# Turning the level tiles of x by transposing DMA transfers on SP instead of PE and DVE

## The reference

```python
x = x + tanh(g_xattn) * xattn(layernorm(x), ctx, ctx)     # softmax with a temperature from a small MLP on score statistics
y = layernorm(x)
# _bitlinear(a, w) = act_quant(a) @ weight_quant(w).T
# act_quant(a): scale = 127 / max|a| of the row; round(a * scale) / scale   (levels from -127 to 127)
# weight_quant(w): levels -1, 0, 1 by the mean of |w|
h = silu(_bitlinear(y, w_gate)) * _bitlinear(y, w_up)      # inner size 1024
x = x + tanh(g_ffn) * _bitlinear(h, w_down)
```

## Time and profile before

| | us |
|---|---|
| median of three runs | 788.13 |
| lowest, highest | 787.66, 788.53 |
| the profiled execution | 786.88 |
| its span from first to last instruction | 785.0 |

### The profile page before, as it was taken

One profiled execution on the slowest core, in us unless ns is written; L12 is line 12 of the kernel. 1 busy time (PEld: TensorE's weight loads), 2 busy tenths in 40 slices (PEclk: granted clock), 3 DMA queues, 4 the chain that ended last, 5 costly groups with the idle time before them and its releaser, 6 DMA issues.

```text
span 785.0 us, 20889 instructions
## 1 busy us (share of the span) xinstructions
PE 707.7 (90%) x7127; PEld 479.5 (61%) x7127; DVE 702.0 (89%) x1432; ACT 672.5 (86%) x1440; POOL 506.1 (64%) x1004
## 2 busy tenths in 40 slices
PE   7557899989999999999999999999999888879896
PEld 5334566767676766666666666676766566634453
DVE  5779799979899999998999999899999887889995
ACT  1469799999999999989999999999999987559884
POOL 4747657667777776766767676767675146546873
PEclk9667599999999999999999999999999999999998
DMA  9897856465567575667565758565755023238887
GB/s 213 191 256 165 189 140 134 115 124 132 138 125 146 123 145 127 147 118 154 118 151 125 151 120 142 125 154 115 153 111 116 13 73 101 67 74 183 184 178 193
DMA packets 148886, 108.49 MB, mean 138 GB/s; under 512 B 56991, under 2 KB 145183, under 8 KB 148767
## 3 DMA queue, kind: packets, MB, share of 16 engines
q1 hardware_dynamic: 143630, 101.98, 59.7%
q10 hardware_dynamic: 5152, 5.19, 2.7%
HBM read 49.54 MB, written 12.85 MB: 79 GB/s over the span
## 4 chain that ended last, share of the span: by engine, by line
PE 46%; ACT 20%; DVE 14%; issue 10%; POOL 7%; DMA 1%; ACTq 1%; SPq 0%; POOLq 0%; DVEq 0%
PE p_m L1458 9%; PE p_o L1380 8%; ACT ex L1228 7%; PE p_s L1360 7%; ACT pt L1218 6%; PE p_t L1401 6%; PE p_m L1439 5%; DVE stats L950 3%; PE p_m L1447 3%; DVE nm L969 2%; PE p_m L1431 2%; ACT L1218 2%; ACT L1254 2%; POOL kst L785 2%; PE p_m L1465 2%
## 5 line engine op out<-in xcount | busy, mean ns | idle before, releaser
L1228 ACT ACTIVATE ex<-p_s,nm 112x375 f32<-112x375 f32 x512 | 275.0, 616 | 12.4 <-DVE nm L969 12.4
L1218 ACT ACTIVATE pt<-p_t,ct 128x336 f32<-128x336 f32 x488 | 244.9, 574 | 29.1 <-PE p_t L1401 26.6
L950 DVE BATCH_NORM_STATS2 stats<-ex 112x6 f32<-112x375 f32 x512 | 252.4, 534 | 1.8 <-ACT ex L1228 1.8
L969 DVE TENSOR_REDUCE nm<-p_s 112x2 f32<-112x750 f32 x256 | 235.9, 922 | 2.3 <-PE p_s L1360 2.2
L1360 PE MATMUL p_s<-kst,qst 96*112 96x375 bf16 x512 | 156.1, 351 | 13.7 <-ACT ex L1228 7.7
L1401 PE MATMUL p_t<-qst,kst 99*128 99x112 bf16 x1464 | 115.3, 214 | 4.9 <-ACT pt L1218 4.2
L1401 PEld LDWEIGHTS p_t<-qst,kst 99*128 99x128 bf16 x1464 | 91.4, 98 | 43.9 <-issue 19.4
L1439 PE MATMUL p_m<-wv_sb,ctxt 128*128 128x256 f32 (+1 forms) x384 | 107.7, 404 | 5.0 <-DVE on L938 3.2
L1380 PE MATMUL p_o<-pt,va 128*32 128x112 f32 (+1 forms) x3072 | 101.6, 265 | 0.5 <-ACT ex L1228 0.5
L1458 PE MATMUL p_m<-ctxt,wk_sb 128*128 128x375 f32 x240 | 94.8, 519 | 1.7 <-DVE qf L918 1.1
L1360 PEld LDWEIGHTS p_s<-kst,qst 96*112 96x112 bf16 x512 | 67.0, 140 | 46.0 <-ACT ex L1228 36.3
(11 more groups left out here) (189 smaller groups left out, 1162.8 us busy)
## 6 DMA issues: line engine op xcount, KB each, us to landing
kst<-kp SPq DMA_DIRECT2D x378, 93.8 KB, 3.5
ctxt<-ctxt_dram SPq DMA_DIRECT2D x32, 375.0 KB, 4.2
qbounce<-qp SPq DMA_DIRECT2D x32, 168.0 KB, 2.5
qst<-qbounce SPq DMA_DIRECT2D x32, 168.0 KB, 3.6
qst<-qbounce SPq DMA_DIRECT2D x32, 112.0 KB, 3.4
xm<-x_dram SPq DMA_DIRECT2D x32, 112.0 KB, 2.3
x_dram<-x SPq DMA_DIRECT2D x32, 112.0 KB, 1.9
xt<-x_dram SPq DMA_DIRECT2D x28, 128.0 KB, 3.2
```

The lines of the kernel that those rows point to most:

```text
L950: last = nc.vector.bn_stats(stats[:, nb % RING, 2 * pb + i], ex[0:SQ, 2 * (t % 2) + i, :])
L969: nc.vector.tensor_reduce(nm[:, n % RING, 2 * p:2 * p + 2], p_s[t % 2][0:SQ, :, 0:SK], axis=AX.X, op=ALU.max, negate=True).then_inc(s_max, 1)
L1218: nc.scalar.activation(pt[:, (2 * r + i) % 8], st_home(r, i)[:, 0:KC * SQ].rearrange("k (c q) -> k c q", c=KC), ACT.Exp, scale=ct[:, nr % ...
L1228: nc.scalar.activation(ex[0:SQ, 2 * ((t - 1) % 2) + i, :], p_s[(t - 1) % 2][0:SQ, i, 0:SK], ACT.Exp, bias=nm[:, ne % RING, h:h + 1]).then_ ...
```

## The change

The PE transposes and the DVE copies of the level tiles are gone. SP issues one transposing transfer for each tile (`turn_group`), straight from `fxq` to `xqt(k)`, at the slot at which PE transposed before, and for the late groups at tiles 14 and 17. It waits for POOL's levels and for what the copy waited for. POOL waits for the landing of a group's transfers before it writes the buffer again. PE's gate product waits for the landing. Since p_t[0] is free in the tail, row 30's `ong` transposes ride there, and rows 30 and 31 have a bank each. Tile 0 stands behind slot 283 instead of 284, and `rows_scale` at slot 280 instead of 282.

```diff
-        last_ride = p_t[1][:, 0:C * SQ].rearrange("p (c q) -> p c q", c=C)
+        last_rides = [p_t[i][:, 0:C * SQ].rearrange("p (c q) -> p c q", c=C) for i in range(2)]
...
-            return last_ride if m5 == B - 1 else tail_ride if t >= TAIL else ride[t % 2]
+            return last_rides[m5 % 2] if m5 >= B - 2 else tail_ride if t >= TAIL else ride[t % 2]
...
-        BETWEEN = {SLOTS * (B + 3) + 4: 0, SLOTS * (B + 3) + 6: 1,
+        BETWEEN = {SLOTS * (B + 3) + 3: 0, SLOTS * (B + 3) + 6: 1,
...
-        VAR_AT, SQRT_AT, RSTD_AT, RSTD_LATE = SLOTS * B + 6, SLOTS * B + 7, SLOTS * (B + 3) + 2, 18
+        VAR_AT, SQRT_AT, RSTD_AT, RSTD_LATE = SLOTS * B + 6, SLOTS * B + 7, SLOTS * (B + 3), 18
...
+            def turn_group(i):
+
+                if i == 0:
+                    sp.wait_ge(s_kp2, count(2, B - 1, 2))
+                    for b in (B - 2, B - 1):
+                        sp.wait_ge(s_kst[b % KRING], ring_count(192, b, KRING))
+                if i == EARLY_GROUPS:
+                    sp.wait_ge(s_vmm, 3 * B)
+                sp.wait_ge(s_gq, count(1, i, 1))
+                for g in range(GROUP):
+                    k = GROUP * i + g
+                    if k >= GROUP * TAILED:
+                        sp.wait_ge(s_u, count(1, k - GROUP * TAILED, 1))
+                    sp.dma_start_transpose(xqt(k), fxq[:, i % 2, g]).then_inc(s_gt[i % 2], 16)
...
+                i = group_at(t, 3)
+                if i is not None:
+                    turn_group(i)
...
+                if s - 4 in LATE_AT:
+                    turn_group(LATE_AT[s - 4])
...
-                    pool.wait_ge(s_gt, count(1, i - 2, 1))
+                    pool.wait_ge(s_gt[i % 2], ring_count(16 * GROUP, i - 2, 2))
...
-                i = group_at(t, 4)
-                if i is not None:
-                    copy_group(i)
...
-            def copy_group(i):
-
-                dve.wait_ge(s_gt, count(1, i, 1))
...
-                    last = nc.vector.tensor_copy(xqt(k), p_xq(i)[:, g])
-                last.then_inc(s_gc, 1)
...
-                    if m5 == B - 1:
-                        pe.wait_ge(s_e2, 2 * SLOTS * B)
-                        pe.wait_ge(s_gc, TAILED)
+                    if m5 >= B - 2:
+                        pe.wait_ge(s_e2, 2 * SLOTS * B - (2 if m5 == B - 2 else 0))
...
-            def transpose_group(i):
-
-                pe.wait_ge(s_gq, count(1, i, 1))
-                if i > 0:
-                    pe.wait_ge(s_gc, count(1, i))
-                for g in range(GROUP):
-                    for c in range(C):
-                        last = nc.tensor.transpose(p_xq(i)[:, g, c, :], fxq[:, i % 2, g, c * P:(c + 1) * P], identb[:, :])
-                last.then_inc(s_gt, 1)
...
-                    pe.wait_ge(s_gc, count(1, n // GROUP, 1))
+                    pe.wait_ge(s_gt[n // GROUP % 2], ring_count(16 * GROUP, n // GROUP, 2))
                     if n == 0:
-                        pe.wait_ge(s_gc, EARLY_GROUPS)
-                        pe.wait_ge(s_otc, B - 1)
+                        pe.wait_ge(s_e1, 2 * SLOTS * B)
+                        pe.wait_ge(s_otc, B - 2)
                         pe.wait_ge(s_fw, 6)
```

More of the change, by code:

```diff
@@ L235, in ride_of @@
         def ride_of(t, m5):
-            return last_ride if m5 == B - 1 else tail_ride if t >= TAIL else ride[t % 2]
-        def p_xq(i):
-            home = p_s[0].ap().bitcast(BF16).rearrange("p b k -> p (b k)") if i < EARLY_GROUPS else p_t[1].ap().bitcast(BF16)
-            return home[:, 0:GROUP * D].rearrange("p (g c r) -> p g c r", g=GROUP, c=C)
+            return last_rides[m5 % 2] if m5 >= B - 2 else tail_ride if t >= TAIL else ride[t % 2]
         s_wk, s_wq, s_w = sem("s_k_weights"), sem("s_q_weights"), sem("s_weights")
@@ L278, in gated_block @@
         s_gl = [sem(f"s_f_x_group{i}") for i in range(2)]
-        s_ag, s_gx, s_gr, s_gq, s_gt, s_gc, s_gs = (sem(f"s_f_x_{i}") for i in ("means", "chain", "rounded", "quant", "transposed", "copied", "scales"))
+        s_ag, s_gx, s_gr, s_gq, s_gs = (sem(f"s_f_x_{i}") for i in ("means", "chain", "rounded", "quant", "scales"))
+        s_gt = [sem(f"s_f_x_transposed{i}") for i in range(2)]
         s_g, s_u, s_sg, s_h, s_hmx, s_hrec, s_hinv, s_hr, s_hq = (sem(f"s_f_{i}") for i in (
@@ L376, in turned @@
             return x if 0 <= x < B else None
-        BETWEEN = {SLOTS * (B + 3) + 4: 0, SLOTS * (B + 3) + 6: 1, SLOTS * (B + 3) + 7: 2, SLOTS * (B + 4) + 1: 3, SLOTS * (B + 4) + 2: 4, SLOTS * (B + 4) + 5: 5, SLOTS * (B + 5) + 4: 6, SLOTS * (B + 6) + 4: 7}
+        BETWEEN = {SLOTS * (B + 3) + 3: 0, SLOTS * (B + 3) + 6: 1, SLOTS * (B + 3) + 7: 2, SLOTS * (B + 4) + 1: 3, SLOTS * (B + 4) + 2: 4, SLOTS * (B + 4) + 5: 5, SLOTS * (B + 5) + 4: 6, SLOTS * (B + 6) + 4: 7}
         X_AT, SQ_AT = TAIL, 9
-        VAR_AT, SQRT_AT, RSTD_AT, RSTD_LATE = SLOTS * B + 6, SLOTS * B + 7, SLOTS * (B + 3) + 2, 18
+        VAR_AT, SQRT_AT, RSTD_AT, RSTD_LATE = SLOTS * B + 6, SLOTS * B + 7, SLOTS * (B + 3), 18
         IDLE = {TILES: 2, TILES + 3: 1}
@@ L1031, in x_group @@
                     last.then_inc(s_gr, 1)
-            def copy_group(i):
-                dve.wait_ge(s_gt, count(1, i, 1))
[L1036 to L1041, removed]
-                for g in range(GROUP):
-                    k = GROUP * i + g
-                    if k >= GROUP * TAILED:
-                        dve.wait_ge(s_u, count(1, k - GROUP * TAILED, 1))
-                    last = nc.vector.tensor_copy(xqt(k), p_xq(i)[:, g])
-                last.then_inc(s_gc, 1)
             def tile(s):
@@ L1053, in tile @@
                     rows_scale(EARLY_TILES, TILES, 1)
-                if s - 6 in LATE_AT:
-                    copy_group(LATE_AT[s - 6])
                 n = s
@@ L1562, in tile @@
                         nc.tensor.matmul(p_u[:, 0, :], identb[:, :], wq8[0][:, 0:512], start=True, stop=True)
[L1563 to L1566, removed]
             timeline(slot, tile)
```

## The result

The changed kernel takes 793.64 us (median of five executions, 790.06 to 797.47) against 787.66 of the kernel before beside it (779.84 to 788.53): a ratio of 1.0113 [1.0077, 1.0149]. A second set of runs gave 795.06 and 1.0126 [1.0088, 1.0165]. By medians it is slower by 6.0 and 8.1 us, by means by 8.2 and 9.1, where I had put the chance of slower at 0.20 and the end of my range at 790.2. The profiled execution took 793.64 us too, with a span of 791.8.

The account below looks back on a forecast made before the run. Near the last attention rows no engine is full; the path passes between DVE, PE and POOL, then DVE bounds from 689.5. -2.34 - 1.50 + 3.65 - 0.40 = -0.6 us on 788.13 gives 787.5; range 784.6 to 790.2.

Parts of the forecast that it names:

- SP's waits cost no load, and only issue time adds up, 1.2 us a group: Transposing transfers on SP: waiting for POOL's quantization delays no load; issue 0.6 us each, landing 2.5; price taken 0.
- Rival D: Transfers land later than two groups of POOL's work, at `quant_group`'s wait on `s_gt`: 0.6 each, four meetings, 789.9 us; chance 0.18.
- The stall: First feed-forward tiles: x2 of row 30 behind tile 0 on DVE, PE's OB waits for it; loss 3.65 us.
- B: Rival, first tiles: PE's clock stays high while OB waits, so loss only 2.25 us; 786.1 us, chance 0.17.
- B2: Rival, first tiles: OB does not wait for DVE's x2, so no loss there; 783.9 us, chance 0.10.
- The upstream gain: Up to the first gate product: vanished copies and transposes on the path give 2.34 us, clock 1.5; total 3.8.
- At 656 to 664 the copies: DVE ahead of `on`: two pairs of copies leave the path, so V0 starts 0.79 us sooner.
- The 0.80 us at 670.6 to 678: DVE ahead of `on`: two more pairs of copies leave the path, gaining 0.80 us.
- The clock: PE at V0: idle time falls from 1.68 to about 1.1 us, clock stays high; gain 1.5 us, bounds 0 and 1.5.
- rival C: PE at 664: clock not lost by that idle time alone, upstream gains only 2.34 us; 789.0 us, chance 0.13.
- Group 11's transposes: PE at 686.05, between row 30's projection and the first gate product: their removal gains 0.42 us.
- The late groups: Groups 12 and 13: one DVE copy at 747.39 saved, 0.40 us; SP's 1.2 us more issue at two tiles is borne.

## Why the prediction was wrong

**The step that failed** is "SP's waits cost no load, and only issue time adds up, 1.2 us a group". Its first half holds: no row shows a load held up by the wait for `s_gq`. The second half treated added issue time as free. I took 0.6 us an issue, nearer the plain one, "since a transfer moves 64 KB", out of the bounds 0.44 and 1.24 that the earlier trace rows give; it is 1.24, the upper one, and 2.46 us a group. And I never asked how much room SP had. A group's loads take 0.93 us and its turning 2.46, and each attention row has four groups to carry; with the row's own work (`xm`, the store, statistics), some 1.5 us, that is 15.1 us of issuing in the 14.6 us which a row lasts. At my 0.6 us an issue it would have been 10.0. The rule is the one used for any engine, and I used it for all but SP, as its row isn't among the busy shares.

**Rival D** had the right place (POOL's wait for a transfer) and the right price of an issue, and the wrong size. It counted each late landing by itself, at most four times 0.6; POOL's waits for a turning are eight and 7.5 us in all. But a full queue carries its delay on: every group comes later than the one before, and it is the loads, which D didn't count, that make the longest waits (2.09, 1.78). POOL's waits for loads and turnings in the rows above are 6.5 us, and 3.6 of them reach row 30.

**The stall** was sized rightly: 3.65 forecast, 4.00 in the profile after, 3.9 by time when done alone. OB started 6.09 us after G (6.1 forecast). Its mechanism is in the rows as the prediction put it (x2 behind the reduce, OB behind x2, low clock); so rivals B and B2 fall.

**The upstream gain** was right only where SP wasn't full. With paired transfers the guard came 2.68 us sooner; the terms up to there were 1.92 and 1.50 for the clock. (One of them, 0.33 for group 5's transposes, is 0.24 by the rule of start to start: 668.95 to 669.19 on PE.) In the changed kernel the four terms gave 0.32 to the end of `on`. At 656 to 664 the copies brought 0.38 instead of 0.79: the row's `on` ended 21.41 us after A instead of 21.79. With the copies gone, the scalings there lie beside POOL's centring and take longer. DVE's and POOL's timelines:

```profile
659.52 0.84 DVE L1043 TENSOR_SCALAR ex<-ex,xinv 128x256 f32<-128x256 f32 x2
...
668.73 0.61 DVE L1043 TENSOR_SCALAR ex<-ex,xinv 128x256 f32<-128x256 f32 x2
...
670.62 0.69 DVE L1034 TENSOR_REDUCE xmax<-ex 128x2 f32<-128x512 f32 x1 [0.97 <-POOL ex L766]
```

```profile
659.58 1.12 POOL L766 TENSOR_SCALAR ex<-ctxt,xinv 128x256 f32<-128x256 f32 x2 [0.20 <-POOL xinv L757]
```

The scaling at 668.73, with no centring beside it, takes 0.61 us, as all do there in the kernel before. The 0.80 us at 670.6 to 678 are lost in the wait of 0.97 us at 670.62, for the centring which itself had waited 2.09 us for a load. So from one `on` to the next it is 14.65 us after and 14.59 before (36.06 less 21.41, 36.38 less 21.79), where 0.33 and 0.80 should have gone.

**The clock** was not regained in the changed kernel, as rival C had it. PE's timeline and two stretches at V0:

```profile
661.04 2.06 PE L1433 MATMUL p_m<-wv_sb,ctxt 128*128 128x256 f32 x4 [1.60 <-DVE on L954]
```

```profile
660.00:662.00 2.00, 0.96 (x2) 0.82 (x3) 0.95 (x3) 0.37 (x1) 1.21 (x3) 0.77 0.35 84
662.00:664.00 2.00, 1.97 (x10) 1.33 (x9) 0.79 (x2) 0.58 (x2) 1.68 (x5) 0.50 0.75 220
```

PE was idle for 1.60 us where I had worked out 1.1: `on` came only 0.38 us sooner, and PE's last product ahead of V0, with no transposes left to do, ended 0.30 us sooner too. All thirteen profiled executions fit the forecast's reason, that a shorter idle time keeps the clock: it was kept, and V0 took 1.13 us, after 1.35, 1.37, 1.38, 1.52, 1.58 and 1.58 us, and lost after 1.60, 1.68, 1.69, 1.70, 1.79, 1.80 and 1.86. So the term failed by its size, and C's reason, a clock lost by more than this idle time, isn't needed at V0. But one execution didn't show how this goes in the changed kernel: of the five executions with its code up to there (two sets, two of tile 0 back, one of late groups on PE) two kept the clock, 1.52 and 1.58. In one of these the guard was no sooner for it (39.80 us after A), in the other 1.0 us (38.81), since it waits for the groups that SP brings late.

**Group 11's transposes**, 0.42 us ahead of the gate product, seem to have brought nothing: guard to G is 7.62 in both. But these two executions had different clocks. Where the projection runs at the low level in both, G starts 1.81 us after it in the changed kernel and 2.27 in the kernel before with tile 0 sooner, so the term came. What hides it is that the execution of the earlier trace rows did a part of its projection at the high level. PE's idle time ahead of the projection did rise, from 0.64 to 2.15 us; that this costs clock isn't shown, since the two other traces of the kernel before (tile 0 sooner, late groups on SP) are at the low level there as well.

**The late groups**: 0.40 us saved on DVE was forecast and 0.15 seen (P1 to Pl). That SP's extra issues are hidden "so that it can bear this" was judged by one tile's due time. The four issues are 4.9 us more, and the tiles that remain work off 2.7 of them; the rest reaches the end as 2.4 us of the profile, of which the times show at most a part.

**`rows_scale` two slots sooner** cost nothing, as forecast.

In all, of +9.5 us in the profiles against -0.6: 3.58 is SP's queue ahead of the guard, 2.41 its backlog at the end, 4.00 the stall (forecast 3.65), and some 3.5 us of upstream gains, clock among them, didn't come (some 0.4 of it only because the two executions had different clocks at the projection).

## What to carry to other kernels

When a step moves to a DMA queue, sum the issue times on that queue over the period of the work, just as for an engine. Do it with the price of the same kind of transfer, not of the same number of bytes, and pair transfers until the sum fits. An order change that lets one tile start sooner has to be read on every engine for what now stands behind that tile. When PE waits ahead of a serial product, look at its granted clock there, in more than one execution: filling that idle time gained 2.2 us here, more than all the turning by DMA did, for which no gain is shown.

## What the runs showed of the hardware

- The issue of a transposing transfer on SP took 1.24 us for 128x256 (64 KB), 1.20 for 128x512 and 1.24 for 128x1024, a plain load 0.44. The landing was 2.4, 2.8 and 3.3 us.
- PE's clock kept the high level (2.4 GHz) over idle times of 1.35 to 1.58 us at V0 (six executions) and fell to the low one (1.2 GHz) over 1.60 to 1.86 us at the same place (seven), and over 3.04 us ahead of the projection. At the transposes of group 10, after 1.63 us in both, the same code was at the high level in one execution (0.40 us for four) and at the low in another (0.61). Four products of the projection took 1.08 or 1.09 us at the high level and 2.02 to 2.05 at the low. Products whose results nobody reads, set into the idle time, kept it high.
- A pair of 128x256 scalings on DVE took 0.84 us and POOL's centring of the same size 1.12 where the two ran at once, and 0.61 and 0.94 where each ran without the other. The kernel before has both cases as well (DVE 0.84 beside POOL 1.09 at 647.3, 0.61 at 659.9). That is read from rows; no run isolates it.
